# Relation rows: 24 tiles move from the first expert stage to the stage that gathers its results

## The chip, the cores and the metric

The kernel runs on one core of a Trainium2 chip. The metric is the device time of one execution in microseconds (us), as the median of several runs. Of the engines, PE multiplies matrices, DVE (VectorE) and ACT (ScalarE) work on tiles, POOL (GpSimd) issues the gathers here, and SP (SyncE) only issues transfers, each engine in the order of its own program. Engines wait for each other through semaphores. Transfers run on 16 DMA engines, whoever issued them.

## The reference

Four layers follow one another on 3125 nodes of 256 numbers: a graph network, a mixture of 16 experts, a second graph network with relations, and a mixture of 8 experts. What matters here:

```
# layer 2: 16 experts, the two best for each node
topk_vals, topk_idx = jax.lax.top_k(gate_logits, K)
h = jax.nn.relu(jnp.einsum('bsh,ehf->bsef', x, w1) + b1)
expert_out = jnp.einsum('bsef,efh->bseh', h, w2) + b2
moe = jnp.sum(topk_w[..., None] * sel, axis=2)
y = x + moe                      # then a layer norm
...
# layer 3: each of 103125 edges takes its source's row times its relation's row
h_src = h_hc[src]
r_uv = r_hc[edge_type]
m = clifford_linear(h_src * r_uv, msg_w, msg_b)
```

## The kernel before

Layer 3 needs one row of 260 numbers for each edge: `r_uv`, already scaled, from a table of 500 relations (`r_table`). The kernel writes these rows in edge order into `relation_rows` in device memory long before layer 3, in the background of earlier stages. The 808 tiles of 128 edges are shared out over the stages by the table `SHARES`; the last entry, 156, is the share of the first expert stage. `RelationRows` does the work in pairs of tiles. `fetch` lets POOL gather two tiles by an indirect DMA (L1555) into one of `RING` buffers, `store` writes a pair out with one DMA (L1563), and a buffer is filled again only when its store has landed. `stored` waits for all stores.

The stages follow each other with a barrier between them: each stage is one `Block`, after which POOL clears the stage's semaphores one by one (L121), and only then does the next stage start.

The first expert stage is `feed_forward` with the prefix `f0` (shown as `f_` in the profile). It runs over 64 tiles of 128 token rows. POOL gathers the rows of a tile (`f_xb`, L2197); PE turns them (`f_pX`), multiplies by the first weights (`f_pH`, L1955) and, after ACT's ReLU, by the second (`f_pY`, L1974); DVE adds the bias (`f_yb`); SP stores the tile to `f_ys` (L1896). SP also loads the weights of a tile whose expert differs from that of two tiles earlier (L1871). For that it reads two numbers from the table `f_etab` for each of its two weight steps in each tile (L1879, L1880, L1888, L1889), and then branches:

```
def second(t, s):
    e = sp.value_load(e_tab[0:1, 0, bass.ds(t, 1)], min_val=0, max_val=ne - 1)
    fresh = sp.value_load(e_tab[0:1, 1, bass.ds(t, 1)], min_val=0, max_val=1)
    sp.wait_ge(s_y, t + 1)
...
with sp.Fori(1, tiles // 2 - 1) as i:
    for s in range(2):
        second(2 * i + s, s)
        if out is None:
            stored(i, s)
        first(2 * i + 2 + s, s)
```

In this stage POOL does the relation rows by itself, with a ring of four pairs (`both`: fetch a pair, store the pair before the last): 12 pairs before its first token gather, then about one pair for each tile, 78 in all.

The next stage is `combine_and_norm`. POOL gathers each node's two results from `f_ys` (`f_got`, L2264): 50 gathers, the last two of them of 53 rows. DVE and ACT add, normalise and write blocks of five tiles into `f_out`, and SP stores each of the five blocks to `h_table` (L2300). After it comes `aggregate` of layer 3 (`agg_r`), which reads `h_table` and `relation_rows`.

Of the kernel before, what the change touches and what calls it, by code (L numbers as in the profile page):

```python
# [25 lines left out]
NJ = NT // J  # L26
# [43 lines left out]
NTP = NT  # L70
MW = NT * P

SHARES = (16, 56, 288, 264, 28, 156)
assert sum(SHARES) == EDGE_TILES
GW = 3 * D + 2
CHUNK = 5
# [93 lines left out]
def constants(nc, c):  # L170

    c.ident = c.sb("ident", [P, P])
    c.ones = c.sb("ones", [P, P])
    c.before = c.sb("before", [P, P])
    c.iota = c.sb("iota", [P, P])
    c.lane = c.sb("lane", [P, 1])
    c.ident_b = c.sb("ident_b", [P, P], BF16)
    c.iota_b = c.sb("iota_b", [P, P], BF16)
    with Core(nc) as k:
        iota_i = k.sb("iota_i", [P, P], I32)  # L180
        lane_i = k.sb("lane_i", [P, 1], I32)
        constants_set(nc, c, iota_i, lane_i, k.sem("const_set"), k.sem("const_iota"))
# [703 lines left out]
def row(ap):  # L886

    return ap.rearrange("(a n) -> a n", a=1).to_broadcast([P, ap.shape[0]])
# [688 lines left out]
def gnn0(nc, c, I, edges, r_table, relation_rows, room, tables):  # L1577
    h_tables = [c.dram(f"h_table{q}", [NTP * P, D]) for q in range(2)]
    x1 = c.dram("x1", [NTP * P, D])
    zh = [c.dram(f"zh{q}", [NTP * P, 2 * D]) for q in range(3)]  # L1580
    folded = c.dram("folded", [2, P, 5 * D])

    def relation(q):
        return r_table, relation_rows, sum(SHARES[:q]), SHARES[q]

    with Core(nc) as k:
        c.tab["a_start"] = k.sb("a_start", [1, STRIPS], I32)
        flat = k.sb("matrix", [P, NT * MW // 4])
        m = flat.bitcast(F8).rearrange("p (q w) -> p q w", q=NT)
        with Core(nc) as kg:  # L1590
            ga = kg.sb("parts0", [P, NT * GW // 2])
            g = ga.bitcast(BF16).rearrange("p (t w) -> p t w", t=NT)
            with Core(nc) as kk:
                c.wide_iota = kk.sb("wide_iota", [P, WIDE])
                c.tile_counts = kk.sb("tile_counts", [P, NT])
                for name, (shape, dt) in tables.items():
                    c.tab[name] = kk.sb(name + "_work", shape, dt)
                prepare_edges(nc, c, I, edges, c.records, r_table, relation_rows, flat, ga)
                gnn0_start(nc, c, I, I["x"], flat, g, zh[0], folded, [relation(0), relation(1)])
            matrix_and_layer(nc, c, c.records, m, g, zh, folded, relation(2))  # L1600
        more_layers(nc, c, m, room, zh, folded, I["x"], relation(3))
    return x1, h_tables, zh[0]
# [646 lines left out]
def gather_results(nc, c, name, k, ys, slot):  # L2249

    k.got = k.sb(f"{name}_got", [P, 2, NT, D])
    k.s_got = [c.pool_sem(f"{name}_got{i}") for i in range(NJ)]
    k.s_rest = k.sem(f"{name}_rest")

    def work(pool):

        pool.memset(k.got[:, :, NT - 1, :], 0.0).then_inc(k.s_rest, 1)
        for i in range(NJ):
            if i == NJ - 1:
                pool.wait_ge(k.s_rest, 1)  # L2260
            for t in range(i * J, i * J + J):
                n = P if t < NT - 1 else TAIL
                for q in range(2):
                    pool.indirect_dma_start(k.got[0:n, q, t, :], None, ys,  # L2264
                                            bass.IndirectOffsetOnAxis(ap=slot[0:n, q, t:t + 1], axis=0)).then_inc(k.s_got[i], 16)

    return work


def combine_and_norm(nc, c, name, I, ys, weight, slot, xn, h_table):  # L2270

    with Core(nc) as k:
        work = gather_results(nc, c, name, k, ys, slot)
        g, b = k.sb(f"{name}_gamma", [P, D]), k.sb(f"{name}_beta", [P, D])
        out = k.sb(f"{name}_out", [P, 2, J, W1])
        clip = k.sb(f"{name}_clip", [P, 2, NT])
# [8 lines left out]
        with nc.Block() as block:  # L2287

            @block.gpsimd
            def _(pool):  # L2290
                work(pool)

            @block.sync
            def _(sp):
                sp.dma_start(g[:, :], row(I["L0_ffn_gamma"])).then_inc(s_gb, 16)
                sp.dma_start(b[:, :], row(I["L0_ffn_beta"])).then_inc(s_gb, 16)
                for i in range(NJ):
                    sp.wait_ge(s_last, i + 1)
                    sp.wait_ge(s_row, (i + 1) * J)
                    sp.dma_start(h_table[i * J * P:(i + 1) * J * P, :].rearrange("(t p) d -> p t d", p=P), out[:, i % 2, :, :])\  # L2300
                        .then_inc(s_saved[i % 2], 16)
                for q in range(2):
                    sp.wait_ge(s_saved[q], 16 * ((NJ + 1 - q) // 2))

# [256 lines left out]
def build(nc, I, out):  # L2561
    with Core(nc) as c:
        c.rdeg = c.sb("rdeg", [P, NTP])
        c.deg = c.sb("deg", [P, 2, NTP])
        c.norm_src, c.norm_dst = c.sb("norm_src", [P, NT]), c.sb("norm_dst", [P, NT])
        c.alive = c.sb("alive", [P, 1])
        c.zero_b = c.sb("zero_b", [P, 512], BF16)
        c.records = c.dram("records", [EDGE_ROWS, 4])
        relation_rows = c.dram("relation_rows", [EDGE_ROWS, W1])
        r_table = c.dram("r1_table", [RT * P, W1])  # L2570
        edges = c.dram("ordered_edges", [EDGE_ROWS, 4], I32)

        c.flags = c.sb("flags", [1, 2], I32)
        c.largest = c.sb("largest", [1, 1])
        c.kinds = c.sb("kinds", [P, EDGE_TILES], I32)
        constants(nc, c)
        tables = {"g_base": ([P, GROUPS], F32), "g_start": ([1, GROUPS], I32), "g_tile": ([1, GROUPS + 1], I32)}
        c.tab = {}
        c.lists = c.dram("edge_lists", [2, EDGE_TILES * P])
        block_tables = {"b_src": ([P, HALVES + EDGES_AT], I32), "b_near": ([P, HALVES + EDGES_AT], F32),  # L2580
                        "b_tile": ([1, HALVES], I32), "b_start": ([1, EDGES_AT], I32)}
        for name, (shape, dt) in block_tables.items():
            c.tab[name + "_d"] = c.dram(name + "_d", shape, dt)
        for name, (shape, dt) in tables.items():
            c.tab[name + "_d"] = c.dram(name + "_d", shape, dt)
        shared = c.sb("parts1_and_x", [P, NT * GW // 2])
        c.x = shared[:, 0:NT * D].rearrange("p (t d) -> p t d", d=D)
        x1, h_tables, zh0 = gnn0(nc, c, I, edges, r_table, relation_rows, shared[:, NT * D:], tables)
        free = NT * D
        for name in ("g_base", "g_start", "g_tile", "b_src", "b_near", "b_start"):  # L2590
            (parts, size), dt = {**tables, **block_tables}[name]
            c.tab[name] = shared[0:parts, free:free + size].bitcast(dt)
            free += size
        c.tab["b_tile"] = c.sb("b_tile", [1, HALVES + 2 * LAG], I32)
        crowded_gnn0(nc, c, I, edges, h_tables, x1, zh0)
        c.xn = c.sb("xn", [P, NT, D])
        logits = [c.sb(f"logits{q}", [P, NT, ne]) for q, ne in enumerate((E0, E1))]
        xn_table = c.dram("xn_table", [NP, D])
        norm_and_gate(nc, c, "ng0", E0, I["L0_ffn_gate_w"], I["L0_ffn_gate_b"], logits[0], xn_table, None,
                      [(c.tab[n][:, :], c.tab[n + "_d"]) for n in ("b_src", "b_near", "b_start")]  # L2600
                      + [(c.tab["b_tile"][:, 2 * LAG:HALVES + 2 * LAG], c.tab["b_tile_d"])],
                      (r_table, relation_rows, sum(SHARES[:4]), SHARES[4]))

        c.h = c.sb("h1", [P, NT, D])
        h1_table = c.dram("h1_table", [NP, W1])

        def finish0(ys, weight, slot, xn):
            combine_and_norm(nc, c, "f0", I, ys, weight, slot, xn, h1_table)

        experts(nc, c, I, "f0", E0, F0, TILES0, False, I["L0_ffn_w1"], I["L0_ffn_b1"], I["L0_ffn_w2"], I["L0_ffn_b2"],  # L2610
                logits[0], xn_table, None, ACT.Relu, finish0,
                (r_table, relation_rows, sum(SHARES[:5]), SHARES[5]))
        gnn1(nc, c, I, relation_rows, h1_table, logits[1], xn_table)

        experts(nc, c, I, "f1", E1, F1, TILES1, True, I["L1_ffn_W1"], I["L1_ffn_b1"], I["L1_ffn_W2"], I["L1_ffn_b2"],
                logits[1], xn_table, (I["L1_ffn_ln_g"], I["L1_ffn_ln_b"]), ACT.Gelu, None, None, out)
# [38 lines left out]
```

## Time and profile before

| | |
|---|---|
| median of 3 runs | 3194.33 us (3190.97 to 3194.51) |
| profiled execution, own time | 3200.53 us |
| its span in the trace | 3198.8 us |
| first expert stage | about 1066 to 1430 us of the span |
| stage that gathers its results | 1431.75 to 1536 us |

The profiled execution took 6.2 us more than the median of the runs; 1.7 us of its time lie outside the span. All times below count from the span's start.

### The profile page before, as it was taken

How to read it: one execution, taken by the hardware profiler on the slowest of the kernel's cores; microseconds unless marked ns; L12 is line 12 of the kernel's file. 1: busy time of each engine (PE TensorE's matmuls, PEld its weight loads, DVE VectorE, ACT ScalarE, POOL GpSimd, SP SyncE). 2: the span in 40 equal slices, each digit the busy share in tenths (PEclk: the TensorE clock that was granted, in tenths of full speed). 3: DMA queues.
4: the chain of work that ended last, by engine and by line, in shares of the span. 5: the costliest groups of instructions: out<-in, count | busy, mean ns of one | idle time of the engine just before them, and what ended most of it. 6: DMA issues, size and time to landing. Idle time of an engine off the chain costs nothing. (4 is left out here: it accounts for less than half of the span.)

```text
span 3198.8 us, 47731 instructions
## 1 busy us (share of the span) xinstructions
PE 2336.8 (73%) x11533; PEld 1763.3 (55%) x11533; DVE 1708.0 (53%) x4536; ACT 1455.5 (46%) x3766; POOL 1993.6 (62%) x1963
## 2 busy tenths in 40 slices
PE   1549999989997398870366666666666666699997
PEld 1226666667686387750244444444444435599996
DVE  6658898857787400017556665566566655410110
ACT  0246677645565133223544444344444434355553
POOL 1647777667775777746577777777777760133332
PEclk9979999999998599995676776777677777799998
DMA  6657777578886666763677777777777752463232
GB/s 215 230 163 217 222 228 214 173 228 263 248 262 212 212 213 218 242 217 99 203 201 207 203 205 204 202 203 204 200 205 202 207 159 77 159 180 90 50 74 64
DMA packets 365416, 605.79 MB, mean 189 GB/s; under 512 B 82338, under 2 KB 235179, under 8 KB 362384
## 3 DMA queue, kind: packets, MB, share of 16 engines
q0 software_dynamic: 101648, 270.35, 31.7%
q1 hardware_dynamic: 244992, 310.17, 30.0%
q10 hardware_dynamic: 18544, 22.59, 2.1%
q8 instruction: 95, 1.56, 0.2%
q14 instruction: 137, 1.12, 0.1%
HBM read 443.45 MB, written 164.32 MB: 190 GB/s over the span
## 5 line engine op out<-in xcount | busy, mean ns | idle before, releaser
L659 POOL DMA_INDIRECT agg_r_rows<-h_table,parts_and_x x832 | 839.0, 1008 | 290.1 <-issue 224.8
L715 PE MATMUL agg_r_sums<-agg_r_rows,agg_r_onehot 128*128 128x257 f32 x1664 | 667.2, 550 | 388.6 <-DVE agg_r_rows L697 346.2
L715 PEld LDWEIGHTS agg_r_sums<-agg_r_rows,agg_r_onehot 128*128 128x128 f32 x1664 | 414.2, 272 | 624.5 <-issue 550.7
L626 ACT ACTIVATE agg_r_gap<-iota,parts_and_x 128x128 f32<-128x128 f32 x832 | 286.7, 392 | 461.4 <-PE agg_r_sums L715 434.9
L697 DVE TENSOR_TENSOR agg_r_rows<-agg_r_rows,agg_r_rel 128x514 f32<-128x514 f32 x416 | 290.7, 699 | 299.3 <-DMA agg_r_rows<-h_table,parts_and_x 298.4
L688 DVE TENSOR_TENSOR acc<-acc,agg_r_sums 128x257 f32 (+1 forms) x836 | 353.5, 423 | 138.6 <-issue 56.8
L1555 POOL DMA_INDIRECT rl_buf<-r_table,kinds x288 | 322.9, 1121 | 132.9 <-issue 73.1
L1955 PE MATMUL f_pH<-f_xT,f_w 128*128 128x128 f32 x2816 | 351.7, 283 | 31.0 <-DMA f_w<-in_L_ffn_w 18.6
L1955 PEld LDWEIGHTS f_pH<-f_xT,f_w 128*128 128x128 f32 x2816 | 336.6, 196 | 63.1 <-issue 24.7
L1974 PE MATMUL f_pY<-f_w,f_hT 128*128 128x256 f32 x1408 | 328.2, 383 | 19.3 <-DMA f_w<-in_L_ffn_w 19.3
L2040 ACT ACTIVATE f_hT<-f_pH,f_b 128x128 f32<-128x128 f32 x704 | 198.3, 373 | 303.8 <-PE f_pH L1955 303.5
L1361 PE MATMUL la_acc<-la_parts,la_counts 128*128 128x512 f32 x1250 | 309.3, 404 | 12.0 <-DVE la_parts L1468 12.0
L1555 POOL DMA_INDIRECT rm_buf<-r_table,kinds x264 | 258.9, 981 | 92.0 <-issue 70.1
L1974 PEld LDWEIGHTS f_pY<-f_w,f_hT 128*128 128x128 f32 x1408 | 260.3, 192 | 54.0 <-DMA f_w<-in_L_ffn_w 22.9
L1361 PEld LDWEIGHTS la_acc<-la_parts,la_counts 128*128 128x128 f32 x1250 | 234.6, 190 | 73.4 <-issue 25.9
L2185 POOL DMA_INDIRECT f_ys<-f_yb,f_home x56 | 88.2, 1574 | 272.7 <-DVE f_yb L2170 264.3
L1275 DVE TENSOR_SCALAR b_oh<-b_numbers,b_code 128x400 bf16<-128x400 f16 x980 | 252.7, 323 | 0.0
L1154 PE MATMUL b_strips<-b_oh,b_at 128*128 128x400 bf16 x980 | 199.1, 334 | 52.9 <-ACT b_at L1224 37.0
L1401 ACT ACTIVATE la_counts<-matrix 128x640 fp32r<-128x640 fp8e4 x250 | 183.9, 737 | 94.9 <-PE la_acc L1361 87.7
L2197 POOL DMA_INDIRECT f_xb<-xn_table,f_token x120 | 118.9, 991 | 162.3 <-DVE f_home L2145 116.2
L2164 DVE TENSOR_TENSOR f_plain<-f_pY,f_b 128x256 f32<-128x256 f32 x56 | 23.8, 425 | 359.4 <-PE f_pY L1974 359.4
L1555 POOL DMA_INDIRECT f_rr_buf<-r_table,kinds x156 | 156.7, 1005 | 57.1 <-issue 42.7
(404 smaller groups left out, 3406.4 us busy)
## 6 DMA issues: line engine op xcount, KB each, us to landing
agg_r_rel<-relation_rows SPq DMA_DIRECT2D x404, 260.0 KB, 3.3
relation_rows<-rl_buf SPq DMA_DIRECT2D x144, 260.0 KB, 3.3
relation_rows<-rm_buf SPq DMA_DIRECT2D x132, 260.0 KB, 3.4
relation_rows<-f_rr_buf POOLq DMA_DIRECT2D x78, 260.0 KB, 2.9
f_w<-in_L_ffn_W SPq DMA_DIRECT2D x28, 512.0 KB, 5.7
f_w<-in_L_ffn_W SPq DMA_DIRECT2D x14, 1024.0 KB, 5.4
agg_r_rows<-h_table,parts_and_x POOLq DMA_INDIRECT x832, 3.5
f_w<-in_L_ffn_w SPq DMA_DIRECT2D x38, 256.0 KB, 4.8
```

The lines of the kernel that those rows point to most:

```text
L626: last = nc.scalar.activation(gap[:, n % HOT, t, :], c.iota[:, 0:P], ACT.Abs, bias=c.tab["b_near"][:, bass.ds(g * 2 + t, 1)])
L659: pool.indirect_dma_start(rows[:, n % SLOTS, t, :], None, table, bass.IndirectOffsetOnAxis(ap=indices[:, t:t + 1], axis=0)).then_inc(s_row ...
L688: v.tensor_tensor(here, here, sums[:, (2 * (n - LAG) + t) % BANKS, 0:used], ALU.add).then_inc(s_acc, 1)
L697: v.tensor_tensor(here, here, rel[:, n % SLOTS, :, 0:used], ALU.mult).then_inc(s_ready, 1)
L715: last = nc.tensor.matmul(sums[:, (2 * n + t) % BANKS, 0:used], onehot[:, n % HOT, t, :], rows[:, n % SLOTS, t, 0:used], start=True, stop= ...
L1154: last = nc.tensor.matmul(strips[:, n % BANKS, 0:CODES], at[:, n % 2, t, :], oh[:, n % 2, t, :], start=t == 0, stop=t == DEEP - 1)
L1275: last = v.tensor_scalar(oh[:, n % 2, t, :], numbers[:, :], code[:, q, 1, own, t:t + 1], None, ALU.is_equal)
L1361: last = nc.tensor.matmul(acc[:, n % 2, :], counts[:, i, j, :], parts[:, s, :], start=s == 0, stop=s == NT - 1)
L1555: pool.indirect_dma_start(self.buf[:, n, g, :], None, self.table, bass.IndirectOffsetOnAxis(ap=self.c.kinds[:, at:at + 1], axis=0)).then_i ...
L1955: last = nc.tensor.matmul(pH[s][:, f * P:(f + 1) * P], w1b[:, s, f // (FC // 2), at:at + P], xT[:, s, h, :], start=h == 0, stop=h == KD - 1)
L1974: last = nc.tensor.matmul(pY[s][:, 0:D], hT[:, s, f, :], w2b[:, s, f, :], start=f == 0, stop=f == FC - 1)
L2040: nc.scalar.activation(hT[:, s, f, :], pH[s][:, f * P:(f + 1) * P], act_fn, bias=b1s[:, bass.ds(e, 1), f]).then_inc(s_hT, 1)
```

## The change

The first expert stage keeps 132 tiles, 66 pairs; the other 24 tiles, 12 pairs, become a share of their own, which `combine_and_norm` works off. There POOL fetches all 12 pairs behind the 50 gathers of the results, into a ring of 12 pairs, so that no fetch waits for a store. SP issues the stores: three pairs ahead of the fourth block's store to `h_table`, six ahead of the fifth's, three behind it, and then waits until all have landed. The ring's 12 store semaphores and one more belong to this stage, so POOL clears them at its end.

```
-SHARES = (16, 56, 288, 264, 28, 156)
+SHARES = (16, 56, 288, 264, 28, 132, 24)
...
         work = gather_results(nc, c, name, k, ys, slot)
+        rel = RelationRows(nc, c, k, f"{name}_rc", *relation, False, 12)
...
             def _(pool):
                 work(pool)
+                rel.fetch(pool, 0, rel.pairs)
...
                 for i in range(NJ):
+                    if i >= NJ - 2:
+                        rel.store(sp, *((0, 3) if i == NJ - 2 else (3, rel.pairs - 3)))
                     sp.wait_ge(s_last, i + 1)
                     sp.wait_ge(s_row, (i + 1) * J)
                     sp.dma_start(h_table[i * J * P:(i + 1) * J * P, :].rearrange("(t p) d -> p t d", p=P), out[:, i % 2, :, :])\
                         .then_inc(s_saved[i % 2], 16)
+                rel.store(sp, rel.pairs - 3, rel.pairs)
+                rel.stored(sp)
...
-            combine_and_norm(nc, c, "f0", I, ys, weight, slot, xn, h1_table)
+            combine_and_norm(nc, c, "f0", I, ys, weight, slot, xn, h1_table, (r_table, relation_rows, sum(SHARES[:6]), SHARES[6]))
```

On POOL, in the loop over the tiles of the first expert stage, before the change (f_xb is a tile's token rows, f_rr_buf the relation buffers):

```order
L2197 DMA f_xb<-xn_table,f_token 128x256
L1555 DMA f_rr_buf<-r_table,kinds 128x260 x2
L1563 DMA relation_rows<-f_rr_buf 128x520
L1555 DMA f_rr_buf<-r_table,kinds 128x260 x2
L1563 DMA relation_rows<-f_rr_buf 128x520
L2197 DMA f_xb<-xn_table,f_token 128x256
```

And the same loop in the changed kernel:

```order
L1555 DMA f_rr_buf<-r_table,kinds 128x260 x2
L1563 DMA relation_rows<-f_rr_buf 128x520
L2197 DMA f_xb<-xn_table,f_token 128x256 x2
L1555 DMA f_rr_buf<-r_table,kinds 128x260 x2
L1563 DMA relation_rows<-f_rr_buf 128x520
```

Before, some token gathers have two pairs behind them and all others one; now every tenth or so has none.

On POOL, in the stage that gathers the results, before (f_got holds the results; L121 are the clears of semaphores at the stage's end):

```order
L2257 MEMSET f_got 128x2x256
L2264 DMA f_got<-f_ys,f_slot 128x256 x48
L2264 DMA f_got<-f_ys,f_slot 53x256 x2
L2287 UNCONDITIONAL_BRANCH
L118 UNCONDITIONAL_BRANCH
L121 ISA x17
```

And in the changed kernel (f_rc_buf is the ring of twelve pairs):

```order
L2264 DMA f_got<-f_ys,f_slot 53x256 x2
L1555 DMA f_rc_buf<-r_table,kinds 128x260 x24
L2288 UNCONDITIONAL_BRANCH
L118 UNCONDITIONAL_BRANCH
L121 ISA x30
```

The 24 gathers stand behind all 50, and there are 13 clears more.

On SP in the same stage, the difference from before (-) to the change (+):

```order
-L2300 DMA h_table<-f_out 128x5x260 x5
-L2287 UNCONDITIONAL_BRANCH
+L2295 UNCONDITIONAL_BRANCH
+L2297 DMA f_gamma<-in_L_ffn_gamma 128x256
+L2298 DMA f_beta<-in_L_ffn_beta 128x256
+L2304 DMA h_table<-f_out 128x5x260 x3
+L1563 DMA relation_rows<-f_rc_buf 128x520 x3
+L2304 DMA h_table<-f_out 128x5x260
+L1563 DMA relation_rows<-f_rc_buf 128x520 x6
+L2304 DMA h_table<-f_out 128x5x260
+L1563 DMA relation_rows<-f_rc_buf 128x520 x3
```

Nine of the twelve stores, each with its wait for the pair's two gathers, stand ahead of a store to `h_table`; three stand behind the last one.

## Rows read from the trace of the kernel before

**Rows 1.** The page: chain of work that ended last, by engine.
```profile
PE 13%; DVE 1%; DMA 0%; issue 0%; ACT 0%; POOLq 0%; ACTq 0%; DVEq 0%
```
**Rows 2.** Busy time by stretch: the expert stage, the gathers, what follows them.
```profile
core 0: us, PE busy (x) PEld busy (x) DVE busy (x) ACT busy (x) POOL busy (x), PEclk, DMA share, GB/s
...
1112.00:1427.00 315.00, 264.89 (x1664) 230.31 (x1664) 26.76 (x63) 99.53 (x384) 227.70 (x264) 0.96 0.71 228
...
1432.00:1501.00 69.00, 0.00 (x0) 0.00 (x0) 53.67 (x159) 20.58 (x45) 53.85 (x51) 0.50 0.39 115
1501.00:1536.00 35.00, 0.00 (x0) 0.00 (x0) 19.52 (x66) 20.28 (x43) 0.00 (x0) 0.50 0.18 60
```
**Rows 3.** Waits of PE from 1111 to 1430: us, times, longest.
```profile
PE f_pY L1974 <- DMA f_w<-in_L_ffn_w: 19.3, 14, 3.0
PE f_pH L1955 <- DMA f_w<-in_L_ffn_w: 18.6, 14, 3.9
PE f_pX L1943 <- DMA f_xb<-xn_table,f_token: 13.1, 1, 13.1
```
**Rows 4.** Waits of SP from 1104 to 1430, all but one of 0.2 us.
```profile
SPq L1868 <- PE f_pH L1955: 8.1, 1, 8.1
SPq L1926 <- DVE f_yb L2140: 4.4, 2, 3.2
SPq L1928 <- DMA f_ys<-f_yb: 1.4, 1, 1.4
```
**Rows 5.** SP's store of a tile, L1896, 1111 to 1430: count, ns, first, last.
```profile
L1896 SPq DMA_DIRECT2D f_ys<-f_yb x62: 342/347/761, 1129.9 to 1422.4; - x62
```
**Rows 6.** The same line from 1250 to 1290.
```profile
L1896 SPq DMA_DIRECT2D f_ys<-f_yb x10: 346/346/363, 1250.5 to 1288.5; - x10
```
**Rows 7.** SP's weight loads, L1871, 1111 to 1430.
```profile
L1871 SPq DMA_DIRECT2D f_w<-in_L_ffn_w x52: 333/342/528, 1121.1 to 1403.0; - x52
```
**Rows 8.** SP's reads of the expert table, L1880, 1121 to 1422.
```profile
L1880 SPq TENSOR_LOAD <-f_etab x61: 262/317/1241, 1125.2 to 1417.9; - x61
```
**Rows 9.** The same line in the second expert stage, 2800 to 3000.
```profile
L1880 SPq TENSOR_LOAD <-f_etab x27: 261/267/286, 2805.4 to 2997.1; - x27
```
**Rows 10.** The relation buffers of the first expert stage, over the whole span.
```profile
L1555 POOL DMA_INDIRECT f_rr_buf<-r_table,kinds x156: 951/957/4261, 1066.2 to 1409.2; - x156
L1563 POOL DMA_DIRECT2D relation_rows<-f_rr_buf x78: 542/587/605, 1074.7 to 1412.4; - x78
...
  issue: 42.7, 140
...
DMA to landing us min/median/max: 2.5/3.2/6.4
```
**Rows 11.** Timeline among the result gathers: start, us, engine, line.
```profile
1481.02 1.48 DVE L2384 TENSOR_TENSOR f_got<-f_got,f_gamma 128x1280 f32<-128x1280 f32 x1
...
1481.75 1.58 POOL L2264 DMA_INDIRECT f_got<-f_ys,f_slot  x1 [0.30 <-issue]
```
**Rows 12.** Timeline from the last result gather to the next stage.
```profile
1499.43 1.56 POOL L2264 DMA_INDIRECT f_got<-f_ys,f_slot  x1 [0.31 <-issue]
...
1521.20 1.49 DVE L2384 TENSOR_TENSOR f_got<-f_got,f_gamma 128x1280 f32<-128x1280 f32 x1 [1.92 <-ACT f_got L2319]
...
1530.51 0.36 SPq L2300 DMA_DIRECT2D h_table<-f_out  x1
...
1536.08 1.02 PE L707 MATMUL agg_r_sums<-zero_b 128*128 128x257 bf16 x4 [109.19 <-PEq L116]
```
**Rows 13.** The page: relation stores issued by SP, median us to landing.
```profile
relation_rows<-rm_buf SPq DMA_DIRECT2D x132, 260.0 KB, 3.4
```
**Rows 14.** Clears of semaphores, L121, 1530 to 1537.
```profile
L121 POOLq EVENT_SEMAPHORE_RANGE_CLEAR  x17: 37/38/38, 1534.7 to 1535.7; - x17
```
**Rows 15.** Transfers from 1334 to 1412: KB each, median us to landing.
```profile
relation_rows<-f_rr_buf POOLq DMA_DIRECT2D x17, 260.0 KB, 4.8
...
f_rr_buf<-r_table,kinds POOLq DMA_INDIRECT x32, 4.9
```

More of the change, by code:

```diff
@@ L71 @@
 MW = NT * P
-SHARES = (16, 56, 288, 264, 28, 156)
+SHARES = (16, 56, 288, 264, 28, 132, 24)
 assert sum(SHARES) == EDGE_TILES
@@ L2267, in gather_results, with combine_and_norm @@
     return work
-def combine_and_norm(nc, c, name, I, ys, weight, slot, xn, h_table):
+def combine_and_norm(nc, c, name, I, ys, weight, slot, xn, h_table, relation):
     with Core(nc) as k:
         work = gather_results(nc, c, name, k, ys, slot)
+        rel = RelationRows(nc, c, k, f"{name}_rc", *relation, False, 12)
         g, b = k.sb(f"{name}_gamma", [P, D]), k.sb(f"{name}_beta", [P, D])
@@ L2291, in _ @@
                 work(pool)
+                rel.fetch(pool, 0, rel.pairs)
             @block.sync
@@ L2297, in _ @@
                 for i in range(NJ):
+                    if i >= NJ - 2:
+                        rel.store(sp, *((0, 3) if i == NJ - 2 else (3, rel.pairs - 3)))
                     sp.wait_ge(s_last, i + 1)
@@ L2301, in _ @@
                         .then_inc(s_saved[i % 2], 16)
+                rel.store(sp, rel.pairs - 3, rel.pairs)
+                rel.stored(sp)
                 for q in range(2):
@@ L2607, in finish0 @@
         def finish0(ys, weight, slot, xn):
-            combine_and_norm(nc, c, "f0", I, ys, weight, slot, xn, h1_table)
+            combine_and_norm(nc, c, "f0", I, ys, weight, slot, xn, h1_table, (r_table, relation_rows, sum(SHARES[:6]), SHARES[6]))
         experts(nc, c, I, "f0", E0, F0, TILES0, False, I["L0_ffn_w1"], I["L0_ffn_b1"], I["L0_ffn_w2"], I["L0_ffn_b2"],
```

## The prediction, made blind

> **What bounds the kernel now.** I began with the chain that ended last. It covers 13% of the span, all in the last expert stage [rows 1], so it says nothing about the stages that the change touches, and I took those by stretch. In the first expert stage no engine is full by busy time: PE 265 us of 315, POOL 228 [rows 2]. But POOL pays some 0.30 us of issue before each instruction (42.7 us over 140 of them [rows 10]), and 264 instructions times 0.30 are 79 us, so POOL has 307 us of work in 315. It looks like the bound, and it is what the change unloads. Whether it is one shows in who waits. PE waited for token rows once, at the start of the stage; its other long waits, 19.3 and 18.6 us, are for weights [rows 3]. POOL's gathers come in time.
>
> Who issues the weights? SP, and SP waited three times worth naming between 1104 and 1430: 8.1 us before its first weight step in the loop, and 4.4 and 1.4 us when the tiles were over [rows 4]. In between it never waited for anybody. An engine that never waits sets the pace. So the loop runs at the speed of SP's own program, and PE's waits for weights are what a late SP looks like from PE. SP's pace is read from its store of a tile: 61 steps from 1129.9 to 1422.4 are 4.80 us for a tile [rows 5], and in a stretch without weight loads 9 steps from 1250.5 to 1288.5 are 4.22 us [rows 6]. Of the 0.58 us between, the 52 loads at 0.342 us [rows 7] explain 52 x 0.342 / 61 = 0.29. The other 0.29 us, 17 us over the stage, I give to SP's instructions being slower while transfers run: a read of the expert table takes 317 ns at the median and up to 1241 here [rows 8], but 267 and at most 286 in the second expert stage, which moves no relation rows [rows 9].
>
> In the next stage POOL is idle for the last 35 us and DMA is busy 18% of them [rows 2]: its last result gather ends at 1499.43 + 1.56 = 1501.0, the last store to the node table is issued at 1530.51, the next stage begins at 1536.1 [rows 12]. That hole is where the 12 pairs go.
>
> **Removed from the expert stage.** 24 gathers and 12 stores, on POOL 12 x (2 x 1.26 + 0.89) = 41 us [rows 10]. Since neither PE nor SP waits for POOL, this is worth nothing by itself. What can be worth something is the traffic: 66 pairs in the loop become 54, 18% less. If the 17 us that SP loses shrink by the same 18%, that is 3 us. From below the bound is nothing (the slow reads may fall together with the weights' own bursts), from above all 17. I take 3, since the tokens' and weights' transfers stay as they are.
>
> The weights could land sooner as well. PE waited 37.9 us for them [rows 3], and 18% of that is 6.9 us. I take none of it, because SP issues the next load no sooner when the last one lands sooner.
>
> The Trainium skill (DMA: Bandwidth & Descriptors, section "Issuing engines are not separate DMA queues") says that transfers of all issuing engines interleave on the same 16 DMA engines and that a sequencer's time to issue is usually small beside the transfer. By that rule the weights' transfers would set the pace, and lighter POOL traffic would gain those 6.9 us or more. The trace speaks against it here, since SP has no idle time in 300 us; it is a rival below.
>
> **Added to the gathering stage.** POOL starts the 24 gathers at 1501.3. Each takes 0.957 + 0.30 = 1.26 us [rows 10], together 30.2, so they end at 1531.5. A gather beside DVE's wide TENSOR_TENSOR took 1.58 us, 0.62 more [rows 11]; that instruction still comes twice, in each of the two last blocks, the last time at 1521.20 [rows 12], so 1.2 us more: the last gather starts at 1531.7 and ends at 1532.7. Gathers and stores of this kind land 3.2 us after their start [rows 10], so the last pair is there at 1534.9. SP's store follows, and lands 3.4 us after issue [rows 13]: 1538.4. Before, the clears began at 1534.7 [rows 14], so this is 3.7 us later. The 17 clears took 1.0 us, 0.06 each; 13 more are 0.8 us. POOL does them alone and the next stage waits for them, so nothing hides them. The sum is 4.5 us. The last store to the node table is in flight as the last gathers are issued, so I take 5. From below: fastest landings seen, 2.5 us [rows 10] for both and no DVE hold, 3.7 - 0.7 - 0.9 - 1.2 + 0.8 = 1.7 us. From above: landings as in the crowded stretch, 4.9 and 4.8 us [rows 15], add 3.1 to 4.5: 7.6.
>
> **Costed at nothing.** The first 11 pairs hide behind DVE's and ACT's two last blocks. The nine stores ahead of the last two node-table stores add waits to SP. Behind the waiting SP are only these stores, and ACT and DVE wait for the earlier ones of them. Pairs 0 to 2 are there by 1501.3 + 6 x 1.26 + 3.2 = 1512, before the fourth block's store. Pair 8 is there by 1501.3 + 18 x 1.26 + 1.2 + 3.2 = 1528.4, 2 us before 1530.5. If that cover is gone, each us comes on to the last node-table store, but that one still lands before pair 11's store unless pair 8 is about 4 us late. The fetches wait for nothing, the ring having twelve places.
>
> **Sum.** 5 - 3 = +2 us. The profiled execution took 3200.53 us, so it would be 3202.5; its 6.2 us over the median of the runs I carry as they are: 3194.3 + 2 = 3196.3 us. About 0.2% (6.4 us) is what a measurement of this kernel can tell from no change, so this is no change.
>
> **The rivals.**
>
> *POOL is the bound.* For it: 307 us of work in 315. Then the 41 us go, less 5: 3158 us. Against it: PE waits once for token rows. 3%.
>
> *The weights' transfers are the bound.* PE's 37.9 us of waits fall by 6.9, or by twice that if POOL, no longer full, also pauses whenever PE stalls: 3194.3 + 5 - 6.9 = 3192, down to 3185.5. For it: the DMA share of 0.71 over the stage [rows 2], and landings of 4.9 us in the crowded stretch [rows 15] instead of 3.2. Against it: SP's row without waits. 15%. The skill's rule quoted above is the reason to look at it.
>
> *POOL's gathers are held up by DVE and the tail grows: slower.* DVE is busy 19.5 of the last 35 us [rows 2]. Were all gathers in that share, 13 of 24, stretched by 0.62 us instead of two, the tail would be 13 x 0.62 - 1.2 = 6.9 us later: 3203 us. It decides from 4.4 us on, seven more stretched gathers, or as much from landings at the crowded figures. For it: the 1.58 us row. Against it: DVE's other instructions there are shorter. 20%. The Trainium skill (GPSIMD Engine Reference, section "Key points") says that GpSimd shares its interfaces to SBUF with VectorE and contends with instructions of two SBUF inputs; most of DVE's here are of that kind, and no row but that of the wide one shows a price for it.
>
> **How the numbers follow.** The forecast has 62%, the rivals 3, 15 and 20. Forecast alone: bounds of +1.7 and +7.6 for the added part, 0 and 6 for the gain, 3190 to 3202. The range of 3189 to 3203 leaves out POOL's case, the deep end of the weights' case and the far end of the slow one. Faster by over 0.2%, below 3187.9: POOL's case and half of the weights', 0.1. Slower, above 3200.7: most of the slow case and a little of the forecast, 0.18. Within: 0.72.
>
> **What would show it.** SP still without a wait in the expert loop, a tile at 4.75 us instead of 4.80, PE's waits for weights near 38 us: the pace is SP's. If the stage shortens by over 7 us, SP's pace was not what I took it for. In the gathering stage: 24 gathers from 1501 us on in that count (shifted by what the expert stage gained), the last ending 31 to 33 us later; the last node-table store at its old distance from the first gather; the clears starting 3 to 5 us later in the stage and taking 1.8 us. I am wrong if SP's stores hold up a node-table store, or if the next stage begins where it did.

## The result and the profile after

| | before | after |
|---|---|---|
| median, first comparison | 3196.41 us (3190.97 to 3202.68, 10 runs) | 3203.48 us (3196.84 to 3210.61, 10 runs) |
| median, second comparison (e5_again) | 3200.91 us (25 runs) | 3205.82 us (12 runs) |
| profiled execution: own time, span | 3200.53, 3198.8 us | 3202.48, 3200.7 us |

The ratio is 1.0022 with a 95% interval of 1.0012 to 1.0032, and the second time 1.0017 (1.0005 to 1.0029). So the change makes the kernel about 0.2% slower, 5 to 7 us. The forecast was 3196.3 us, no change. 3203.48 lies half a us above the range.

Whole spans of single profiles do not show this: they differ by 1.9 us, since the layer-3 stage that follows took 1104.4 us in the one and 1100.4 in the other, with the same code. I therefore compare stages, each from the last clear of semaphores (L121) of the stage ahead to its own last clear. The expert stage took 366.3 us before and 366.3 after; the gathering stage 104.3 before (1431.4 to 1535.7) and 111.4 after (1433.8 to 1545.2).

**The expert stage.** Waits of SP from 1104 to 1434 in the kernel after (us in total, times, longest), to be held against [rows 4]:

```profile
SPq L1868 <- PE f_pH L1955: 9.0, 2, 8.5
SPq L1926 <- DVE f_yb L2140: 4.5, 2, 3.3
SPq L1928 <- DMA f_ys<-f_yb: 1.4, 1, 1.4
SPq L1896 <- DVE f_yb L2140: 0.3, 1, 0.3
SPq L1868 <- PE f_pY L1974: 0.3, 1, 0.3
```

Left out are a wait of 36.7 us for the expert table ahead of the loop and one of 0.2 us. The rest are the rows of before with 1.6 us added, 0.9 of it in the first row: in the loop SP still waits for hardly anybody. Its store of a tile (L1896), with count, ns, first and last start:

```profile
L1896 SPq DMA_DIRECT2D f_ys<-f_yb x62: 348/352/868, 1132.9 to 1424.4; - x62
```

61 steps in 291.5 us are 4.78 us for a tile, against 4.80 in [rows 5]. PE's waits for weights in the same stretch, beside [rows 3]:

```profile
PE f_pY L1974 <- DMA f_w<-in_L_ffn_w: 16.5, 10, 3.0
PE f_pH L1955 <- DMA f_w<-in_L_ffn_w: 15.1, 8, 4.0
```

That is 31.6 us, where it was 37.9, but the fall is not owed to the change: the same kernel's second profile (e5_again) has 38.5.

```profile
PE f_pY L1974 <- DMA f_w<-in_L_ffn_w: 21.5, 11, 3.1
PE f_pH L1955 <- DMA f_w<-in_L_ffn_w: 17.0, 11, 4.2
```

What differs is PE itself. The windows from the first to the last tile store, in before, after and e5_again (columns as in [rows 2]):

```profile
1129.90:1422.40 292.50, 248.46 (x1573) 216.10 (x1572) 25.91 (x61) 93.62 (x362) 213.76 (x248) 0.97 0.72 229
...
1132.90:1424.40 291.50, 254.64 (x1577) 222.83 (x1576) 25.90 (x61) 93.77 (x366) 184.36 (x214) 0.94 0.67 208
...
1130.40:1420.60 290.20, 247.57 (x1570) 216.76 (x1570) 25.90 (x61) 92.23 (x360) 183.73 (x213) 0.96 0.67 209
```

In the profile of after the granted clock (mean of the window, 1 being full speed) was 0.94 instead of 0.97, PE was busy 6.2 us longer, and it waited 6.3 us less for weights, while the steps took as long. A slower PE only met the weights later; it did not set the pace.

Where POOL's freed 41 us went is the first of its waits:

```profile
POOL f_xb L2197 <- PE f_pX L1943: 49.8, 18, 7.3
```

POOL waits to overwrite token rows that PE has not yet turned. In the kernel before the same wait came to 12.7 us in 10 times. POOL got done sooner and stood before PE, which stood before SP.

**The gathering stage.** The windows that answer to [rows 2] (PE, PEld, DVE, ACT, POOL busy, PEclk, DMA share, GB/s):

```profile
1115.00:1429.00 314.00, 271.97 (x1664) 238.06 (x1664) 26.75 (x63) 98.46 (x384) 196.05 (x227) 0.92 0.67 207
1434.00:1503.00 69.00, 0.00 (x0) 0.00 (x0) 53.97 (x159) 20.74 (x45) 53.67 (x51) 0.50 0.39 115
1503.00:1545.50 42.50, 0.00 (x0) 0.00 (x0) 19.69 (x66) 20.36 (x43) 25.70 (x25) 0.50 0.62 200
```

The DMA share of what was the quiet hole rose from 0.18 to 0.62. The timeline from the last result gather on, beside [rows 12]:

```profile
1501.51 1.56 POOL L2264 DMA_INDIRECT f_got<-f_ys,f_slot  x1 [0.31 <-issue]
...
1503.37 0.96 POOL L1555 DMA_INDIRECT f_rc_buf<-r_table,kinds  x1 [0.30 <-issue]
...
1514.74 1.48 DVE L2390 TENSOR_TENSOR f_got<-f_got,f_gamma 128x1280 f32<-128x1280 f32 x1
...
1514.93 2.12 POOL L1555 DMA_INDIRECT f_rc_buf<-r_table,kinds  x1 [0.30 <-issue]
...
1523.91 1.77 POOL L1555 DMA_INDIRECT f_rc_buf<-r_table,kinds  x1 [0.30 <-issue]
...
1526.61 5.77 SPq L1563 DMA_DIRECT2D relation_rows<-f_rc_buf  x6
...
1532.65 0.38 SPq L2304 DMA_DIRECT2D h_table<-f_out  x1
...
1534.84 5.29 SPq L1563 DMA_DIRECT2D relation_rows<-f_rc_buf  x3
1535.06 0.95 POOL L1555 DMA_INDIRECT f_rc_buf<-r_table,kinds  x1 [0.30 <-issue]
...
1545.63 1.02 PE L707 MATMUL agg_r_sums<-zero_b 128*128 128x257 bf16 x4 [116.62 <-PEq L116]
```

From the start of the last result gather to the next stage's first matmul it is 44.1 us, and was 36.6. The clears beside [rows 14], and DMA issues from 1532 on (last number: median us to landing):

```profile
L121 POOLq EVENT_SEMAPHORE_RANGE_CLEAR  x30: 37/38/38, 1543.0 to 1545.2; - x30
```

```profile
h_table<-f_out SPq DMA_DIRECT2D x1, 650.0 KB, 5.9
f_rc_buf<-r_table,kinds POOLq DMA_INDIRECT x4, 5.0
```

The last 650 KB store to the node table and the last four gathers are in flight together, and the gathers take 5.0 us to land (median), where the forecast took 3.2.

### The profile page after: what moved, and what is told of

Same layout as the page of the kernel before. It is cut to its first block and busy times, and to the rows that moved or that the text cites. A ratio compares the mean times of both kernels' runs of the same rounds, so it can differ in the third digit from the quotient of the medians.

```text
span 3200.7 us, 47738 instructions
## 1 busy us (share of the span) xinstructions
PE 2343.5 (73%) x11533; PEld 1765.0 (55%) x11533; DVE 1709.7 (53%) x4536; ACT 1454.4 (45%) x3766; POOL 1985.3 (62%) x1951
## 5 line engine op out<-in xcount | busy, mean ns | idle before, releaser
L1555 POOL DMA_INDIRECT rl_buf<-r_table,kinds x288 | 322.9, 1121 | 133.7 <-issue 75.0
L2140 DVE TENSOR_TENSOR f_yb<-f_pY,f_b 128x256 f32<-128x256 f32 x64 | 27.2, 425 | 295.1 <-PE f_pY L1974 246.9
```

The lines of the kernel that those rows point to most:

```text
L1555: pool.indirect_dma_start(self.buf[:, n, g, :], None, self.table, bass.IndirectOffsetOnAxis(ap=self.c.kinds[:, at:at + 1], axis=0)).then_i ...
```

## Experiments

My theory: SP's program sets the pace of the expert stage, so unloading POOL there is hidden, and the added tail costs 7 us. Rivals: the weights' transfers are the bound, POOL is the bound, or the 7 us come from somewhere else than the tail. The first four kernels ran on one chip with 29 runs of the kernel before (3201.43 us), the last four on another with 25 (3200.91 us).

**The removal alone (e1_less).** The 24 tiles leave the expert stage and do not come back.

```
-SHARES = (16, 56, 288, 264, 28, 156)
+SHARES = (16, 56, 288, 264, 28, 132, 24)
...
+                for at in range(EDGE_TILES - 24, EDGE_TILES, 8):
+                    to = min(at + 8, EDGE_TILES)
+                    sp.dma_start(by_tile[:, at:to, :], none_rows[:, 0:to - at, :]).then_inc(s_stored, 16)
...
```

> The expert stage does 132 tiles of relation rows as in the change, but nobody does the other 24: their rows are set to zero by three stores of SP in the first stage, so their edges count nothing in layer 3. The gathering stage is that of before. Theory (SP's own program sets the pace of the expert stage, which lasted 364.5 us between two stages' clears): 0 to 3 us shorter, 361.5 to 364.5. Rival, the weights' transfers set it: 7 to 14 us shorter. Rival, POOL sets it: 41 us shorter. The whole time carries 3 to 9 us more for the three stores, so the stage's own length is what tells.

Measured: 3198.01 us, ratio 0.9986 (0.9976 to 0.9995), 2 to 8 us faster. The expert stage took 365.2 us, the gathering stage 104.2 as before. The line of SP's tile store (L1900 here) spans 289.5 us, 3.0 less than before:

```profile
L1900 SPq DMA_DIRECT2D f_ys<-f_yb x62: 348/352/388, 1133.6 to 1423.1; - x62
```

So 41 us of POOL's work gone are worth 1.2 us by the stage and 3.0 by this line. POOL as the bound falls; the weights' case, which wanted 7 us or more, does not get them either.

**The addition alone (e2_added).** The expert stage keeps all 156 tiles, and the last 24 are done a second time in the gathering stage, by the changed kernel's `combine_and_norm`.

```
-            combine_and_norm(nc, c, "f0", I, ys, weight, slot, xn, h1_table)
+            combine_and_norm(nc, c, "f0", I, ys, weight, slot, xn, h1_table, (r_table, relation_rows, sum(SHARES) - 24, 24))
```

> The expert stage does all 156 tiles as before, and the gathering stage does the last 24 of them a second time, in the changed kernel's way. Theory (the change's cost is the tail of the gathering stage: last gathers, last stores, 13 clears more): that stage lasts 111 us instead of 104, the expert stage is unchanged, the time is 7 us longer than before, as long as the change. If the change loses by something else, a later stage or the expert stage, this is within 3 us of before.

Measured: 3208.42 us, ratio 1.0016 (1.0005 to 1.0026). The gathering stage took 111.2 us, 6.9 more than before. The gathering stage's growth is as large as the whole loss, without anything taken from the expert stage. The expert stage, with the same code as before, took 368.7 us this time against 366.3: single profiles of one stage differ by that much.

**One more read on SP (e3_read).** Nothing is moved; SP reads one number more for each tile and doesn't use it.

```
                 def second(t, s):
+                    if out is None:
+                        sp.value_load(e_tab[0:1, 0, bass.ds(t, 1)], min_val=0, max_val=ne - 1)
                     e = sp.value_load(e_tab[0:1, 0, bass.ds(t, 1)], min_val=0, max_val=ne - 1)
```

> Before, with one more read of the expert table by SP in each of the first expert stage's tiles, whose result nobody uses. Theory (SP's program sets the pace): a read with its address and check is about 0.58 us, so 62 of them make the stage 30 to 40 us longer. Rivals, POOL or the weights' transfers set the pace: SP's 0.58 us hide in its slack, 0 to 5 us longer.

Measured: 3230.20 us, ratio 1.0084 (1.0066 to 1.0102). The expert stage took 399.0 us, 32.7 more, and the tile store spans 323.7 us, so each tile took 0.51 us longer:

```profile
L1898 SPq DMA_DIRECT2D f_ys<-f_yb x62: 342/352/376, 1133.7 to 1457.4; - x62
```

The extra read takes 0.58 us of SP's program (in one tile of this trace it begins at 1264.97 us, the next read at 1265.55). So a read that feeds nothing comes on the clock with 0.51 of its 0.58 us; on an engine with slack it would have been hidden.

**Sixteen tiles, all stores early (e4_sixteen).** As the change, but with 16 tiles and a ring of eight, every store issued ahead of the last node-table store.

```
-SHARES = (16, 56, 288, 264, 28, 132, 24)
+SHARES = (16, 56, 288, 264, 28, 140, 16)
...
-                        rel.store(sp, *((0, 3) if i == NJ - 2 else (3, rel.pairs - 3)))
+                        rel.store(sp, *((0, 3) if i == NJ - 2 else (3, rel.pairs)))
...
-                rel.store(sp, rel.pairs - 3, rel.pairs)
```

> The change with 16 tiles moved instead of 24, a ring of eight, and all eight stores ahead of the last store to the node table: the last gather ends about 10 us earlier, so its store lands before that of the node table. Theory (the tail costs): the gathering stage lasts 0.6 to 2 us longer than before (nine clears more), the expert stage 0 to 2 us less, the time is within 2 us of before. If the cost is in the gathers or stores themselves, two thirds of the change's loss stay: 4 to 5 us slower.

Measured: 3198.32 us, ratio 0.9991 (0.9979 to 1.0004), 3 us below before by the medians, where within 2 had been expected, but not apart from no change. The gathering stage took 105.2 us, 0.9 more than before, and that is the clears: 26 of them took 1.9 us instead of 1.0 for 17, and they began at the old distance from the last result gather (35.2 us). Its transfers from 1520 on:

```profile
h_table<-f_out SPq DMA_DIRECT2D x2, 650.0 KB, 3.7
relation_rows<-f_rc_buf SPq DMA_DIRECT2D x5, 260.0 KB, 4.2
f_rc_buf<-r_table,kinds POOLq DMA_INDIRECT x6, 2.8
```

With nothing of POOL's in flight beside the last node-table store, the cover holds. The expert stage took 370.4 us here, 4 more than before; 0 to 2 less had been expected. The profiled execution, at 3207.47 us, lies 9 us above the median of this kernel, so I read no loss from it; in it the granted clock over the tile steps was 0.94 as in after, and SP waited 4.8 us for PE and DVE in the loop.

**The change again (e5_again).**

> The changed kernel once more, unchanged, beside the next three. If its loss is the gathering stage's 7 us, it is 5 to 8 us slower than before again, with that stage at 111 us; if the first measurement was partly luck of the expert stage or of layer 3, whose lengths differ by 2 to 8 us between profiles of the same code, it is 1 to 4 us slower.

Measured: 3205.82 us, 1.0017 as told above; expert stage 364.9, gathering stage 111.7 us.

**Almost no relation rows (e6_none).** The expert stage keeps the 12 pairs ahead of its loop, and none in it.

```
-SHARES = (16, 56, 288, 264, 28, 156)
+SHARES = (16, 56, 288, 264, 28, 24, 132)
...
+                for at in range(EDGE_TILES - 132, EDGE_TILES, 8):
+                    to = min(at + 8, EDGE_TILES)
+                    sp.dma_start(by_tile[:, at:to, :], none_rows[:, 0:to - at, :]).then_inc(s_stored, 16)
...
```

> The expert stage does only 24 tiles of relation rows, all of them ahead of its loop, so that no relation rows move beside the loop at all; the other 132 tiles are set to zero by 17 stores of SP in the first stage, so their edges count nothing in layer 3. SP's loop is that of before. Theory (SP's program sets the pace, and relation traffic only slows its reads): the stage loses the slow reads, 15 to 25 us, and keeps SP's 4.2 to 4.4 us for a tile. Rival, the weights' transfers: PE's 38 us of waits go and the stage is 40 us shorter or more, down to PE's own 3.9 us for a tile. Rival, POOL: 60 us shorter. The whole time carries some 20 to 60 us more for the stores in the first stage.

Measured: 3210.31 us, ratio 1.0028 (1.0016 to 1.0039), because the filling with zeros makes the first stage 23.5 us longer; what counts here is the expert stage, 350.9 us, 15.4 less. Waits of SP (without the one for the expert table), of PE for weights and of POOL for PE from 1112 to 1440:

```profile
SPq L1872 <- PE f_pH L1959: 8.3, 1, 8.3
SPq L1930 <- DVE f_yb L2144: 4.5, 2, 3.3
SPq L1932 <- DMA f_ys<-f_yb: 1.4, 1, 1.4
```

```profile
PE f_pY L1978 <- DMA f_w<-in_L_ffn_w: 22.6, 15, 2.5
...
PE f_pH L1959 <- DMA f_w<-in_L_ffn_w: 8.5, 6, 3.5
```

```profile
POOL f_xb L2201 <- PE f_pX L1947: 212.8, 60, 7.4
```

POOL has next to nothing to do and waits 212.8 us for PE, and SP still never waits in the loop. Its tile store spans 276.4 us, 4.53 us for a tile, and the reads of the table (L1884 here) are back at 268 ns, as quiet as the 267 of [rows 9]:

```profile
L1884 SPq TENSOR_LOAD <-f_etab x61: 260/268/1162, 1151.8 to 1428.2; - x61
```

The prediction had split 4.80 into 4.22, 0.29 for the weight loads and 0.29 for reads slowed by traffic. Without the relation traffic 4.53 is left, 4.22 + 0.29 and 0.02; the 4.2 to 4.4 expected for this run had left out the weight loads. SP's 242 reads of the table over the 61 steps, added up in the trace, took 83.6 us before and 67.9 here. Relation rows in the loop therefore cost 16.1 us, 15.7 of them in SP's reads.

**SP relieved (e7_once).** Nothing is moved; SP's loop is written out, and each tile's two numbers are read once instead of twice.

```
                 def second(t, s):
-                    e = sp.value_load(e_tab[0:1, 0, bass.ds(t, 1)], min_val=0, max_val=ne - 1)
-                    fresh = sp.value_load(e_tab[0:1, 1, bass.ds(t, 1)], min_val=0, max_val=1)
+                    if out is None:
+                        e, fresh = read.pop(t)
...
-                with sp.Fori(1, tiles // 2 - 1) as i:
-                    for s in range(2):
-                        second(2 * i + s, s)
-                        if out is None:
+                if out is None:
+                    for i in range(1, tiles // 2 - 1):
+                        for s in range(2):
+                            second(2 * i + s, s)
```

> Before, with SP's loop over the expert stage's tiles written out, and each tile's two numbers of the expert table read once instead of twice, so that SP needs 1.2 us or more less for a tile. Theory: SP no longer sets the pace, and the next to do so is POOL with 302 us of issues in a 312 us loop: the stage is 8 to 15 us shorter. If the weights' transfers set the pace already, 0 to 3 us.

Measured: 3186.96 us, ratio 0.9952 (0.9936 to 0.9969). The expert stage took 354.6 us, 11.7 less. Waits of SP and of PE from 1104 to 1420:

```profile
SPq L1868 <- PE f_pY L1986: 88.3, 59, 7.1
```

```profile
PE f_pX L1955 <- DMA f_xb<-xn_table,f_token: 35.2, 10, 13.6
...
PE f_pY L1986 <- DMA f_w<-in_L_ffn_w: 2.2, 2, 1.2
PE f_pH L1967 <- DMA f_w<-in_L_ffn_w: 1.7, 2, 1.4
```

Now SP waits for PE in nearly every tile, PE's waits for weights are down from 37.9 to 3.9 us, and PE waits ten times for token rows, which POOL gathers: 13.6 us at the start as before, 21.6 us in nine waits in the loop. With SP out of the way POOL is the next to set the pace. How much is owed to the reads and how much to the loop without its own branch and its address arithmetic, this kernel does not tell apart.

**SP relieved, and the change (e8_once_moved).** The two edits together.

> The same loop of SP with the change's 24 tiles moved. Theory: now that POOL is the bound, its 41 us less count, until PE and the weights' loads are next: the expert stage is 20 to 40 us shorter than before, the gathering stage 7 us longer, the whole 13 to 30 us faster than before and 5 to 20 us faster than the same loop without the move. If SP was not what hid the move's gain, this is 7 us slower than the same loop without it.

Measured: 3167.47 us, ratio 0.9891 (0.9874 to 0.9909): 33 us faster than before, 3 more than I had expected at most, and some 20 faster than e7_once. The expert stage took 327.7 us, 38.6 less than before and 26.9 less than with e7_once; the gathering stage 111.7. Waits of PE from 1104 to 1393, and the windows of the loop in e7_once and here (columns as above):

```profile
PE f_pX L1955 <- DMA f_xb<-xn_table,f_token: 13.7, 1, 13.7
PE f_pY L1986 <- DMA f_w<-in_L_ffn_w: 6.8, 12, 1.2
PE f_pH L1967 <- DMA f_w<-in_L_ffn_w: 4.6, 5, 1.1
```

```profile
1115.00:1410.00 295.00, 259.81 (x1657) 229.25 (x1658) 26.34 (x62) 99.42 (x384) 226.16 (x262) 0.95 0.75 241
...
1115.00:1388.00 273.00, 253.72 (x1655) 223.84 (x1656) 26.34 (x62) 98.97 (x384) 196.41 (x227) 0.97 0.74 239
```

PE waits for token rows only once again, as before, and is busy 254 of 273 us. The DMA engines are as busy as in e7_once (0.74 and 0.75), which speaks for POOL's work, and not the load on the DMA engines, as what had held up the rows. PE's busy time fell by 6 us too, at a granted clock of 0.97 instead of 0.95; the two parts of the gain are not separated. The same move that loses 5 to 7 us behind a slow SP gains 20 when SP is not in the way. Of all kernels that ran, this is the fastest.

## Why the prediction was wrong

| us, by stage | expert stage | its 61 tile steps | gathering stage |
|---|---|---|---|
| all 156 tiles: before, e2_added | 366.3, 368.7 | 292.5, 294.5 | 104.3, 111.2 |
| 132 tiles: after, e5_again, e1_less | 366.3, 364.9, 365.2 | 291.5, 290.2, 289.5 | 111.4, 111.7, 104.2 |

**SP's program sets the pace: right.** In the loop SP waits for next to nothing with the change, and for nothing with hardly any POOL work at all (e6_none); an idle read of 0.58 us on it costs 0.51 us for each tile (e3_read), and taking reads from it gives time back (e7_once).

**The gain of 3 us in the expert stage: fits, but is not shown.** The mean of the tile steps falls from 293.5 to 290.4 us, 3.1 less; of the stage from 367.5 to 365.5, 2.0 less. In the one profile of after alone it looks like 1 us or nothing, and profiles of one code differ by 2 us; e4_sixteen, with 16 tiles fewer, had 370.4. The source of the gain is shown: the 17 us of slow reads, of which 18% was taken, were 16 in e6_none. PE's waits for weights were to stay near 38 and were 31.6, 38.5 and 33.5 us in after, e5_again and e1_less; the low one belongs to the lower clock told above.

**The 5 us added in the gathering stage: wrong, and this is the step that failed.** It measured 7.1 by the stages (6.9 in e2_added, 7.4 in e5_again) and 7.5 from the last result gather, against a worked-out sum of 4.5. The term that was too small in every profile is the landing of the last gather: 3.2 us were taken, and 4.5 to 5.8 measured. Laid over the timeline of before by the start of the last result gather, 2.08 us later in after:

- *The gathers.* The last was to start at 1531.7 (24 x 1.26 and 1.2 add up to 1531.5), and started at 1533.0, 1.3 later. One stretched gather for each of the two last blocks was expected (1.2 us); five were stretched, two of them to 2.12 and 1.77 us, together 2.7 us. Part of this stood in the trace of before: behind the gather of 1.58 us in [rows 11] comes a second stretched one, since each block has two wide TENSOR_TENSOR, and another block has one of 1.84.

```profile
1483.63 1.22 POOL L2264 DMA_INDIRECT f_got<-f_ys,f_slot  x1 [0.30 <-issue]
...
1497.28 1.84 POOL L2264 DMA_INDIRECT f_got<-f_ys,f_slot  x1 [0.30 <-issue]
```

- *The last gather's landing.* 3.2 us were taken, 4.7 measured: 1.5. In e4_sixteen, where the gathers are over before the last node-table store, they land in 2.8 (median).
- *The last store and the way to the clears.* The prediction set the landing of this store against the start of the clears of before, as if nothing lay between. The store was issued at 1539.8, and SP's last wait for a landing was over by 1541.8, after 2.0 us where 3.4 were taken; then 1.2 us passed until the clears at 1543.0. That the two together, 3.3 us, came out as the 3.4 was luck.

```profile
L1574 SPq EVENT_SEMAPHORE  x5: 17/28/28, 1540.2 to 1541.8; - x5
```

- *The clears.* 2.2 us for 30, against 1.8: 0.4. They follow each other at 0.064 us, as the 17 of before did, and once in after there is a hole of 0.3 us; e2_added has no hole, and its 30 clears took 1.9.

4.5 + 1.3 + 1.5 - 0.1 + 0.4 = 7.6, and 7.5 were measured. The crowded landing of 4.9 us was in the prediction, but as the upper bound alone. I had seen the 650 KB store in flight at that moment and gave it half a us, and it was worth three times that.

The split between gathers and landing holds for this profile only. In e5_again the gathers were stretched less (1.77 us at most) and the last one started 32.5 us after the last result gather instead of 33.6, but it took 5.8 us to land instead of 4.7 (first line e5_again, second after):

```profile
f_rc_buf<-r_table,kinds POOLq DMA_INDIRECT x1, 5.8
...
f_rc_buf<-r_table,kinds POOLq DMA_INDIRECT x1, 4.7
```

In after, e2_added, e5_again and e8_once_moved alike its rows were there 38.0 to 38.3 us after the last result gather, where the forecast had 35.5, whenever the gather had started. That points to the transfers in flight, the 650 KB store among them, and not to DVE as what held the last pair; no run separates the two.

**Costed at nothing: right, with less to spare than thought.** The last node-table store came 1532.65 - 1501.51 = 31.14 us after the start of the last result gather, and 1530.51 - 1499.43 = 31.08 before. SP's waits for pairs held up no store. But the last of the six stores of pairs ahead of it, which waits for pair 8, was issued by 1526.61 + 5.77 = 1532.38, 0.3 us before it, where the pair had been put 2 us before it.

**The sum.** Measured by its terms it is 7 - 3 = +4 us, with the 3 not shown beyond the spread; that is inside the range given to the forecast but not on its middle. (The 6 us that the range allowed the gain had no row behind them; the text gave 3, and 17 as the bound.) The whole time says +7.1 once and +4.9 once, with intervals of about 4 to 10 and 2 to 9. Of the 7.2 us between 3196.3 and 3203.5, 2.1 are the starting point: the kernel before, taken at 3194.3 from three runs, had a median of 3196.4 beside the kernel after, and 3200.9 and 3201.4 later. 2 are the tail that was too small, and the other 3 lie within these intervals.

**The rivals.** *POOL is the bound* falls (e1_less, e6_none). *The weights' transfers* fall too: e6_none takes all relation traffic from the loop, yet PE still waits 31.1 us for weights and SP for nothing, while e7_once leaves the traffic as it is and PE's waits fall to 3.9. The rule of the Trainium skill (DMA: Bandwidth & Descriptors, section "Issuing engines are not separate DMA queues") is that a sequencer's time to issue is small beside the transfer. The trace agrees: SP's issue of a weight load takes 0.34 us [rows 7], and the load 4.9 us to land in the crowded stretches. What set the pace is the program around the issues, reads and branches included, 4.5 to 4.8 us for a tile, so the prediction drew more from the rule than it says. *The tail grows* is the one whose time came: 6.9 us were worked out for it. Its mechanism has a part of the credit at most, since stretched gathers brought 1.3 us more in after and, by the landings above, perhaps nothing that counted; as much or more came from the landing that I had named there as the other way to the same end. What stood against it, that DVE's other instructions are shorter, overlooked the second wide one of each block. 20% was too little for it.

## What to carry to other kernels

Before work is moved off an engine that looks full, look for the engine that never waits: as long as that one is not relieved, the move only turns busy time into waiting, and once it is, the same move may be worth many times as much (here 20 us instead of a loss). When work is put into a hole at the end of a stage, follow its last piece to the last landing and the last clear, with the landing times of a crowded stretch if any large store is in flight there. A few us of change in a kernel whose runs spread by 20 us are read from stage lengths of several profiles and from many runs, not from two spans.

## What the runs showed of the hardware that was not expected

- A read of one number by SP takes 0.58 us of its program (e3_read): the load is 0.27 us in quiet (e6_none), the rest its address, check and moves. Beside the relation rows' gathers and stores such loads slow down, and over 61 tiles that came to 16 us (83.6 against 67.9 us of loads).
- A gather on POOL beside DVE's wide f32 TENSOR_TENSOR took up to 2.12 us instead of 0.96, where [rows 11] had shown 1.58 and the trace of before has up to 1.84.
- A gather of 128 rows issued while a 650 KB store is in flight took 4.5 to 5.8 us to land (after, e2_added, e5_again, e8_once_moved), and 2.8 (median of six) when the gathers were over before the last such store (e4_sixteen).
- Clearing semaphores between stages took 0.064 us each, for 17 as for 30, with one hole of 0.3 us in four of the five profiles with more than 17. Thirteen more are 0.8 to 1.2 us that nothing hides.
